# Scores of the first 128 queries as plain fp32 matmuls instead of three products of rounded parts

## What is computed

```python
q = jnp.einsum('qdh,bcd->bhcq', Q, x) * sq
k = jnp.einsum('qdh,bcd->bhcq', K, x) * sq
v = jnp.einsum('vdh,bcd->bhcv', V, x) * sv
att = jnp.einsum('bhcq,bhCq->bhcC', q, k) / d_query
att = jnp.where(causal, att, -jnp.inf)
p = jax.nn.softmax(att, axis=-1)
y = jnp.einsum('bhcC,bhCv->bhcv', p, v)
```

## Time and profile before

| | |
|---|---|
| median of 3 runs | 1300.69 us (1300.5 to 1302.07) |
| the profiled execution, its own time | 1301.22 us |
| its span, first to last instruction | 1299.5 us |
| mean granted TensorE clock | 0.992 |
| busy: PE, weight loads, VectorE, ScalarE, GpSimd | 1234.2, 1073.3, 1030.9, 1025.2, 588.2 us |

### The profile page before, as it was taken

One profiled execution on the slowest core, in us unless ns is written; L12 is line 12 of the kernel. 1 busy time (PEld: TensorE's weight loads), 2 busy tenths in 40 slices (PEclk: granted clock), 3 DMA queues, 4 the chain that ended last, 5 costly groups with the idle time before them and its releaser, 6 DMA issues.

```text
span 1299.5 us, 39139 instructions
## 1 busy us (share of the span) xinstructions
PE 1234.2 (95%) x11395; PEld 1073.3 (83%) x11395; DVE 1030.9 (79%) x4814; ACT 1025.2 (79%) x3426; POOL 588.2 (45%) x913
## 2 busy tenths in 40 slices
PE   5799977899999999999999999999999999999996
PEld 4688966778888888888888888888888888888885
DVE  6888879877778787878787887878787877787774
ACT  4866657578888888888888888888888888888883
POOL 4722247534444444444444444444444444444443
PEclk9999989999999999999999999999999999999999
DMA  8000000000000000000000000000000000000000
GB/s 216 1 2 0 1 2 1 1 2 2 3 10 0 8 1 8 0 8 0 8 0 8 0 8 0 8 0 8 0 8 0 8 0 8 0 8 0 9 2 18
DMA packets 14445, 11.83 MB, mean 9 GB/s; under 512 B 852, under 2 KB 12664, under 8 KB 14200
## 3 DMA queue, kind: packets, MB, share of 16 engines
q1 hardware_dynamic: 14240, 11.19, 3.2%
q10 hardware_dynamic: 152, 0.00, 0.0%
HBM read 7.00 MB, written 4.19 MB: 9 GB/s over the span
## 4 chain that ended last, share of the span: by engine, by line
PE 85%; DVE 5%; issue 3%; POOL 2%; ACT 2%; DMA 1%; SPq 1%; DVEq 0%; POOLq 0%; ACTq 0%
PE ps L1110 16%; PE ps L1141 14%; PE ps L1124 12%; PE ps L1150 9%; PE ps L1095 6%; PE ps L1096 5%; PE ps L1097 4%; PE ps L1132 2%; PE ps L1131 2%; PE ps L1130 2%; PE ps L973 1%; PE ps L995 1%; PE ps L1072 1%; PE ps L1051 1%; POOL rstd L318 1%
## 5 line engine op out<-in xcount | busy, mean ns | idle before, releaser
L797 ACT ACTIVATE pr<-ps,neg_max 128x128 f32<-128x128 f32 (+1 forms) x1024 | 426.2, 432 | 119.5 <-DVE neg_max L536 119.5
L333 POOL TENSOR_TENSOR pr<-pr,rinv 128x256 f32<-128x256 f32 x256 | 157.7, 616 | 555.0 <-DVE rinv L544 555.0
L536 DVE CUSTOM_DVE_ANT_0 ps<-ps,mask 128x128 f32<-128x128 f32 (+1 forms) x1024 | 329.1, 388 | 3.4
L335 POOL TENSOR_TENSOR pr<-pr,rinv 128x512 f32<-128x512 f32 x256 | 266.6, 1041 | 0.0
L551 DVE COPY pT<-ps 128x512 f32<-128x512 f32 x256 | 175.3, 685 | 100.1 <-PE ps L1124 100.1
L797 ACT ACTIVATION_READ_ACCUMULATOR pr<-ps,neg_max 128x1 f32 x1024 | 219.1, 214 | 0.0
L1124 PE MATMUL ps<-ident,pr 128*128 128x128 f32 x1536 | 210.2, 273 | 3.8 <-DVE pT L551 1.9
L1124 PEld LDWEIGHTS ps<-ident,pr 128*128 128x128 f32 x1536 | 179.1, 141 | 23.0 <-POOL pr L335 4.3
L1141 PE MATMUL ps<-pT,space 128*64 128x256 f32 (+1 forms) x2048 | 194.9, 332 | 0.7 <-ACT pT L806 0.5
L1141 PEld LDWEIGHTS ps<-pT,space 128*64 128x64 f32 x2048 | 126.8, 136 | 55.0 <-ACT pT L806 0.7
L1095 PE MATMUL ps<-x_hi,wqk_hi 128*128 128x256 f32 x512 | 168.5, 329 | 0.4 <-ACT qk_raw L770 0.3
(11 more groups left out here) (182 smaller groups left out, 2640.7 us busy)
## 6 DMA issues: line engine op xcount, KB each, us to landing
out<-x_all SPq DMA_DIRECT2D x16, 256.0 KB, 2.3
x_all<-L_attn_x SPq DMA_DIRECT2D x1, 768.0 KB, 6.7
x_all<-L_attn_x SPq DMA_DIRECT2D x1, 512.0 KB, 4.6
space<-L_attn_Q SPq DMA_DIRECT2D x1, 512.0 KB, 15.6
space<-L_attn_K SPq DMA_DIRECT2D x1, 512.0 KB, 9.6
space<-L_attn_V SPq DMA_DIRECT2D x1, 512.0 KB, 11.5
space<-L_attn_W SPq DMA_DIRECT2D x1, 512.0 KB, 12.1
dft_s<-dft SPq DMA_DIRECT2D x1, 192.0 KB, 2.6
```

Source lines behind the costliest of these rows:

```text
L333: nc.gpsimd.tensor_tensor(pr[:, buf, :, 0, :], pr[:, buf, :, 0, :], r[:, :, 0:1].to_broadcast([P, 2, P]), ALU.mult)
L335: nc.gpsimd.tensor_tensor(pr[:, buf, :, 1:3, :].rearrange("p h b k -> p h (b k)"), pr[:, buf, :, 1:3, :].rearrange("p h b k -> p h (b k)") ...
L536: last = nc.vector.tensor_tensor_reduce(o, o, mask[:, T - w:T], -1.0, -MASKED, ALU.add, ALU.min, neg_max[:, j, 2 * h + qt:2 * h + qt + 1])
L797: last = nc.scalar.activation(dst, ps[:, BANK_S + 2 * j + h, qt * P:qt * P + w], ACT.Exp, bias=neg_max[:, j, at:at + 1], scale=-1.0, accum ...
```

## The change

The first 128 queries no longer go through rounded parts. Their scores are one plain fp32 matmul per head on the unrounded q and k, row half by row half (K = 64). For even pairs these are read from `qk_raw`; for odd pairs ScalarE now also copies the first 128 query columns and the first 128 key columns from PSUM to a new buffer `qk_odd`. The rounded parts are made for 384 columns (second 128 queries, all 256 keys) and no longer for 512. `qk_raw` is now read by TensorE too, so its writer also waits for `s_done`.

```diff
-        qk_raw = sb("qk_raw", [P, 2 * T])
-        qk_hi = sb("qk_hi", [P, 2, 2, T], F32R); qk_lo = sb("qk_lo", [P, 2, 2, T], F32R)
+        qk_raw = sb("qk_raw", [P, 2 * T]); qk_odd = sb("qk_odd", [P, 2, P])
+        qk_hi = sb("qk_hi", [P, 2, P + T], F32R); qk_lo = sb("qk_lo", [P, 2, P + T], F32R)
...
-                nc.vector.tensor_tensor(qk_lo[:, j].rearrange("p s k -> p (s k)"), qk_raw[:] if j == 0 else ps[:, BANK_QK, :],
-                                        qk_hi[:, j].rearrange("p s k -> p (s k)").bitcast(F32), ALU.subtract).then_inc(qklo_ready, 1)
+                nc.vector.tensor_tensor(qk_lo[:, j], qk_raw[:, P:] if j == 0 else ps[:, BANK_QK, P:],
+                                        qk_hi[:, j].bitcast(F32), ALU.subtract).then_inc(qklo_ready, 1)
...
                 if above_0(n - 1):
                     act.wait_ge(qklo_ready, count(n - 1))
+                    act.wait_ge(s_done, count(2 * n - 2))
                 nc.scalar.copy(qk_raw[:], ps[:, BANK_QK, :]).then_inc(qk_out, 1)
...
-                nc.scalar.copy(qk_hi[:, 0].rearrange("p s k -> p (s k)"), qk_raw[:]).then_inc(qkhi_ready, 1)
+                nc.scalar.copy(qk_hi[:, 0], qk_raw[:, P:]).then_inc(qkhi_ready, 1)
...
-                nc.scalar.copy(qk_hi[:, 1].rearrange("p s k -> p (s k)"), ps[:, BANK_QK, :]).then_inc(qkhi_ready, 1)
+                nc.scalar.copy(qk_odd[:], ps[:, BANK_QK, :].rearrange("p (s k) -> p s k", s=2)[:, :, 0:P])
+                nc.scalar.copy(qk_hi[:, 1], ps[:, BANK_QK, P:]).then_inc(qkhi_ready, 1)
...
-                for qt in range(2):
-                    w = (qt + 1) * P
-                    for k, (q, key) in enumerate(((qk_hi, qk_hi), (qk_hi, qk_lo), (qk_lo, qk_hi))):
-                        for h in range(2):
-                            of_head = slice(h * DQ, (h + 1) * DQ)
-                            last = mm(ps[:, BANK_S + 2 * j + h, qt * P:qt * P + w], q[of_head, j, 0, qt * P:(qt + 1) * P],
-                                      key[of_head, j, 1, 0:w], start=(k == 0), stop=(k == 2), skip_group_check=True)
-                            if qt == 1 and k == 2:
-                                last.then_inc(s_done, 1)
+                for h in range(2):
+                    of_head = slice(h * DQ, (h + 1) * DQ)
+                    q, key = (qk_raw[of_head, 0:P], qk_raw[of_head, T:T + P]) if j == 0 else (qk_odd[of_head, 0, :], qk_odd[of_head, 1, :])
+                    mm(ps[:, BANK_S + 2 * j + h, 0:P], q, key, start=True, stop=True, skip_group_check=True)
+                for k, (q, key) in enumerate(((qk_hi, qk_hi), (qk_hi, qk_lo), (qk_lo, qk_hi))):
+                    for h in range(2):
+                        of_head = slice(h * DQ, (h + 1) * DQ)
+                        last = mm(ps[:, BANK_S + 2 * j + h, P:P + T], q[of_head, j, 0:P], key[of_head, j, P:],
+                                  start=(k == 0), stop=(k == 2), skip_group_check=True)
+                        if k == 2:
+                            last.then_inc(s_done, 1)
```

## The result

| | before | after |
|---|---|---|
| median | 1301.03 us (4 runs) | 1286.51 us (1285.85 to 1286.58, 4 runs) |
| ratio | | 0.9885, 95% interval 0.9871 to 0.9898 |
| profiled execution, its span | 1301.22, 1299.5 us | 1286.5, 1284.8 us |
| busy PE, VectorE, ScalarE | 1234.2, 1030.9, 1025.2 | 1211.6, 995.5, 1031.6 |

A forecast was written before the change was run, and what follows sets the result against it. TensorE alone was taken to bound p = 2 and p = 4, a TensorE-ScalarE loop p = 6 and p = 0. 2 x 0.224 + 2 x 0.09 = 0.63 us a batch, 20.2 over 32: 1280.5 us, range 1273 to 1291.

The forecast's parts named there:

- TensorE's part: Score calls: each loses one step, 0.112 us; 256 calls make 28.7 us, the most the change can bring.
- Rivals 2 (skewed): Score calls: heads skewed by one step, TensorE gains nothing; +1.3 us, 1302; chance 0.07.
- 3 (one after the other, or moving columns as the price): Score calls: plain passes one after another, +22.7 us, 1323; or columns set steps, about +11 us, 1312; together chance 0.07.
- The two kinds of iteration: p = 2 and p = 4 bound by TensorE, -0.224 us each; p = 6 and p = 0 by a TensorE-ScalarE loop, -0.09 each.
- The wait for L799: p = 6 and p = 0: TensorE's wait for the exponentials ahead of the second score call grows, in 44 places.
- ScalarE's +0.02: ScalarE, per iteration: two casts lose 128 columns each, -0.23 us; the copy to qk_odd adds 0.25; net +0.02.
- Rival 1: ScalarE's added copy counts 0.39 us, not 0.25; p = 6 and p = 0 +0.05 each; -11 us, 1289.5; chance 0.12.
- p = 2 is bound by TensorE alone: Iteration p = 2: exponentials have 0.59 us of slack, so both score calls' savings count, -0.224 us.
- What stood close behind the loop: p = 6 and p = 0: ScalarE free 0.10 us before the values; its VectorE path covered; `products` has 0.15 left.
- the narrower one, 1276 to 1286: Forecast's own range: 0.10 to 0.13 us a call and 0 to 0.05 for ScalarE give 15 to 25 us.

The follow-up runs named there:

- the odd half alone: Against the kernel before, only odd pairs get the plain fp32 matmul, with ScalarE's added copy; even pairs as before: 1299.53 us, ratio 0.9995.
- two products: Kernel before, with only the third product (low q by high k) left out for the first 128 queries: 1285.19 us, ratio 0.9875.
- the even pairs only: Against the kernel before, only even pairs get the plain fp32 matmul, read from qk_raw; no added copy: 1290.03 us, ratio 0.9914.
- the run with the values later: Changed kernel with the values' copy moved behind qk_high_even on ScalarE in p = 6 and p = 0: 1285.6 us, ratio 0.9879.
- the run with the heads apart: Changed kernel with head 0's plain matmul first in a score call and head 1's last: 1288.3 us, ratio 0.9903.
- the run with the copy on VectorE: Changed kernel with the copy to qk_odd on VectorE instead of ScalarE, behind qk_hi and ahead of the odd subtraction: 1282.61 us, ratio 0.9863.

## Why the prediction was right, and where it was 6 us off

- **TensorE's part was right.** A call lost one step: 0.89 to 0.78 us, the heads side by side, and the two calls of p = 4 went from 1.57 to 1.34. Rivals 2 (skewed) and 3 (one after the other, or moving columns as the price) are out by the timeline of the call.
- **The two kinds of iteration were right.** p = 6 and p = 0 are a loop over ScalarE, where the first call's saving is lost: the doubled copy cost 0.27 there and nothing elsewhere, leaving it out gave 0.28 back, and the odd half alone made p = 6 longer. The wait for L799 grew at 44 places, as said.
- **The first mis-sized term: ScalarE's +0.02.** It measured +0.06: 0.26 for the copy, and 0.10, not 0.115, for each cast that lost 128 columns. The loop gave 0.04 an iteration in place of 0.09 (in alternate batches of p = 0 more, 0.11; the prediction had read a batch of the other kind). That is 0.06 a batch less than forecast, some 2 us in all. Rival 1, the copy at 0.39, would have given +0.05 here; it went neither that way nor quite mine.
- **The second: "p = 2 is bound by TensorE alone".** I checked its slack at one place, the exponentials (0.59 us), and not at the wait for `x_lo`, where none was left. p = 2 gave 0.17 to 0.21 and not 0.224, with two products only 0.12; some 1 us. p = 4 gave 0.21.
- The rest, about 2 us, stays open: 32 batches times the 0.51 us that a batch got shorter are 16.3 us, and 14.5 were measured. It is of the size in which the loop's entry differs between executions of one kernel (2 us between the changed kernel's two profiles). But chance need not be all of it: the other kernels fall short of 32 times their batch in the same direction, for instance 10.9 us for 12.8 with the even pairs only and 15.7 for 18.0 with two products.
- **What stood close behind the loop was right in the prediction** (ScalarE free 0.10 before the values; the run with the values later finds the loop over VectorE at 7.45 us, 0.09 behind), and wrong in the expectations of the later runs, which took about 7.3 for it.
- **What the range held by.** 1286.5 lies in the stated range of 1273 to 1291, but just outside the narrower one, 1276 to 1286, that the prediction works out from its own terms: ScalarE's +0.06 lies outside the 0 to 0.05 allowed there. The wide range had been opened for rival 1. Both mis-sized terms lie on the same side, so no error cancelled another.

## What to carry to other kernels

A view that has TensorE busy 99% of the time can hide a loop through another engine: compare the same instructions in different iterations of the chain, and a stretch that is longer in some of them names the loop. In a loop over several engines, price what the change adds on each engine in it, and look at every wait of each iteration, not at the tightest-looking one. When half of a change pays for the other, take them apart: here the odd pairs' copy ate most of what their matmuls saved, until it was moved to an engine and a moment in which nobody waited.

## What the runs showed of the hardware

- In the run with the heads apart, matmuls with K = 64 on the two row halves ran as two independent lanes, plain fp32 beside `fp32r` included, and started out of program order across the halves (806.86 before 807.06). The Trainium skill ("TensorE: Matmul & The Clock Gate", Part 3, The mechanism) has matmuls start strictly in program order; here the measurement differs and decides.
- A short wait in the stream costs more than itself. In the run with the copy on VectorE the chain holds 0.04 us of wait ahead of the second call of p = 0, and its plain couples then took 0.49 us of the chain where they take 0.22 when they follow at once. The weight load behind the wait starts together with its matmul, at 802.93; in the call that follows at once it starts at 810.68 and its matmul at 810.79, so that it runs beside the matmuls of the call before. The two stretches on the chain:

```profile
802.93 0.49 PE ps L1111 x4
...
810.96 0.22 PE ps L1111 x4
```

- In the changed kernel's profile a standstill of 2.32 us was followed by a stretch at a granted clock of 0.50, in which steps of `qk_product` took 0.21 us where they take 0.12. A standstill of 1.49 us in the same program was not, and neither was one of 2.40 us in the run with the copy twice.
